# Style steps spread over ScalarE, gamma's last steps on GpSimd and one z tile on VectorE, in an adapter and mixture-of-experts kernel

## The reference

```python
# layer 0: an adapter, chosen per sample
hidden = gelu(x @ down_W.T + down_b)
hidden = hidden @ expert_W[id].T + expert_b[id] + domain_emb[id]
x1 = layernorm(hidden @ up_W.T + up_b + x) * ln_gamma + ln_beta
# layer 1
h = layernorm(x1) * ln_g + ln_b
h_norm = (h - mean_over_tokens(h)) * rsqrt(var_over_tokens(h) + 1e-8)
se = subj_emb[subject_ids]
hyp = relu(se @ hyp_w1 + hyp_b1) @ hyp_w2 + hyp_b2
sty = relu(hyp @ sty_w1 + sty_b1) @ sty_w2 + sty_b2
gamma, beta = split(sty, 2)
h = h_norm * (softplus(gamma) + 1e-8) + beta
# top 2 of 8 experts; each expert: relu(h @ w1 + b1) @ w2 + b2, 128 -> 512 -> 128
out = x1 + sum over experts of gate * expert(h)
```

## Time and profile before

| | |
|---|---|
| median of 3 runs | 119.39 us (118.95 to 119.65) |
| the profiled execution | 119.94 us, span of its program 118.2 us |
| PE busy | 112.0 us (95%) |
| DVE busy | 91.8 us (78%) |
| ACT busy | 84.3 us (71%) |
| POOL busy | 54.1 us (46%) |
| chain that ended last | PE 72%, DVE 14%, ACT 5%, DMA 3%, POOL 1% |

### The profile page before, as it was taken

One profiled execution on the slowest core, in us unless ns is written; L12 is line 12 of the kernel. 1 busy time (PEld: TensorE's weight loads), 2 busy tenths in 40 slices (PEclk: granted clock), 3 DMA queues, 4 the chain that ended last, 5 costly groups with the idle time before them and its releaser, 6 DMA issues.

```text
span 118.2 us, 1665 instructions
## 1 busy us (share of the span) xinstructions
PE 112.0 (95%) x519; PEld 84.3 (71%) x519; DVE 91.8 (78%) x228; ACT 84.3 (71%) x153; POOL 54.1 (46%) x75
## 2 busy tenths in 40 slices
PE   6799988999999999999999999999999999999990
PEld 2157534777777888688888888888888888888780
DVE  4486988999899989997685959595867777776772
ACT  2139845698999988697878787878778687878400
POOL 5020889226417000101259999976758941322310
PEclk9999999999999999999999999999999999999999
DMA  4939699994000000326999300000000000000005
GB/s 68 343 97 365 173 374 442 384 412 150 0 0 3 0 6 0 89 100 165 415 446 408 169 0 6 0 0 0 0 0 0 0 0 0 6 0 0 0 0 178
DMA packets 4473, 14.17 MB, mean 120 GB/s; under 512 B 561, under 2 KB 1905, under 8 KB 4209
## 3 DMA queue, kind: packets, MB, share of 16 engines
q1 hardware_dynamic: 3024, 9.67, 21.9%
q0 software_dynamic: 1008, 3.67, 8.8%
q10 hardware_dynamic: 432, 0.73, 2.2%
HBM read 13.52 MB, written 0.56 MB: 119 GB/s over the span
## 4 chain that ended last, share of the span: by engine, by line
PE 72%; DVE 14%; ACT 5%; issue 3%; DMA 3%; POOL 1%; DVEq 0%; ACTq 0%; POOLq 0%
PE bank L594 22%; PE bank L595 22%; PE bank L633 12%; PE bank L613 11%; DMA ids_i<-ids_dram 3%; DVE x L913 2%; ACT hid_high L508 2%; DVE stats L920 1%; ACT bank L511 1%; DVE hid_low L1005 1%; DVE bank L905 1%; POOL z L370 1%; PE bank L750 1%; DVE stats L876 1%; PE bank L583 1%
## 5 line engine op out<-in xcount | busy, mean ns | idle before, releaser
L508 ACT ACTIVATE hid_high<-bank,early_sb 128x512 fp32r<-128x512 f32 x64 | 44.2, 691 | 15.9 <-PE bank L613 15.8
L1005 DVE TENSOR_TENSOR hid_low<-bank,hid_high 128x512 fp32r<-128x512 f32 x51 | 34.8, 687 | 16.7 <-ACT bank L511 16.1
L511 ACT ACTIVATE bank<-bank,early_sb 128x512 f32<-128x512 f32 x51 | 33.6, 658 | 0.0
L308 POOL TENSOR_TENSOR w_low<-w_raw,w_high 128x256 fp32r<-128x256 f32 x32 | 22.7, 734 | 12.3 <-DMA w_high<-w_all_dram 4.4
L633 PE MATMUL bank<-hid_low,w_high 128*128 128x512 f32 x64 | 25.9, 405 | 0.4 <-DVE hid_low L1010 0.2
L594 PE MATMUL bank<-h_high,w_low 128*128 128x512 f32 x64 | 25.5, 398 | 0.3 <-ACT h_high L486 0.3
L594 PE MATMUL bank<-hid_high,w_low 128*128 128x512 f32 x64 | 25.6, 400 | 0.0
L595 PE MATMUL bank<-h_high,w_high 128*128 128x512 f32 x64 | 25.3, 396 | 0.0
L613 PE MATMUL bank<-h_low,w_high 128*128 128x512 f32 x64 | 25.1, 397 | 0.0
L595 PE MATMUL bank<-hid_high,w_high 128*128 128x512 f32 x64 | 25.0, 390 | 0.0
L318 POOL TENSOR_TENSOR y_sum<-y_sum,y_part 128x512 f32<-128x512 f32 x9 | 11.6, 1292 | 17.3 <-DVE y_part L1025 15.1
(11 more groups left out here) (136 smaller groups left out, 99.2 us busy)
## 6 DMA issues: line engine op xcount, KB each, us to landing
w_high<-w_all_dram POOLq DMA_DIRECT2D x7, 512.0 KB, 7.9
w_raw<-w_all_dram SPq DMA_DIRECT2D x1, 2560.0 KB, 10.9
gate_all<-gate_scratch SPq DMA_DIRECT2D x4, 512.0 KB, 5.9
gate_all<-gate_scratch SPq DMA_DIRECT2D x1, 2048.0 KB, 12.5
w_raw<-w_all_dram SPq DMA_DIRECT2D x3, 512.0 KB, 3.9
style_sb<-style_dram SPq DMA_DIRECT2D x1, 324.0 KB, 5.6
tables_sb<-tables_dram ACTq DMA_DIRECT2D x1, 272.0 KB, 3.8
xT_sb<-xT_dram SPq DMA_DIRECT2D x1, 256.0 KB, 4.4
```

Of the source, the lines that this page charges most:

```text
L308: nc.gpsimd.tensor_tensor(w_low[:, e % W_RING, quarter(q)], w_raw[:, e, quarter(q)], w_high[:, e % W_RING, quarter(q)].bitcast(F32), ALU.s ...
L508: ac(hid_high[:, slot, :], hid_ps[slot][:, :], ACT.Relu, bias=bias).then_inc(relu_steps, 1)
L511: ac(hid_ps[slot][:, :], hid_ps[slot][:, :], ACT.Relu, bias=bias).then_inc(relu_steps, 1)
L1005: v.tensor_tensor(low, ps, high.bitcast(F32), ALU.subtract).then_inc(low_vector, 1)
```

## The change

Four things are changed; all else is as before.

- Style: the steps of hyp1 and hyp2 go from VectorE to ScalarE. ScalarE now takes hyp1, weight quarter 0, hyp2, quarter 1, sty1, quarter 2, gamma_raw, and rounds quarter 3 only behind the soft logarithm. On VectorE the one step left, se_T, is behind `token_mv(0, 0, HB)`, and `centre(1)` and `adapter_out(1)` are ahead of `x1_stats(0)`.
- gamma: ScalarE writes a second tile, gamma_relu = max(g, 0). GpSimd does the rest of the softplus in four small steps, behind its z tiles and ahead of quarter 3 of expert 0. VectorE's t_gain waits for all four (`gamma_steps`).
- z: tile 3 (`normalise(T + 1)`) is made on VectorE instead of ScalarE.
- ScalarE's order behind gamma_raw: the root of sample 0, gamma_relu, beta_T, the root of sample 1, then the soft exponential and logarithm. minus_abs waits for gamma_raw alone.

```diff
@@ gpsimd
+            def softplus():
+                pool.wait_ge(gamma_relu_ready, 1)
+                pool.wait_ge(soft_ln, 1)
+                nc.gpsimd.tensor_tensor(gamma_T[:, :], gamma_relu[:, :], soft[:, 2, :], ALU.add).then_inc(gamma_steps, 1)
+                pool.wait_ge(gamma_steps, 1)
+                nc.gpsimd.tensor_scalar(gamma_T[:, :], gamma_T[:, :], 1e-8, None, ALU.add).then_inc(gamma_steps, 1)
+                pool.wait_ge(gamma_steps, 2)
+                nc.gpsimd.tensor_scalar(minus_gamma[:, :], gamma_T[:, :], -1.0, None, ALU.mult).then_inc(gamma_steps, 1)
+                nc.gpsimd.tensor_scalar(gamma_g[:, :], gamma_T[:, :], col(C_LNG), None, ALU.mult).then_inc(gamma_steps, 1)
...
-            split_lows(0)
+            split_lows(0, (0, 1, 2))
             normalise(0, T)
+            softplus()
+            split_lows(0, (3,))
             split_lows(1, (0, 1))
@@ scalar
             token_root(0, tiles(0, 2))
-            round_first_weights((0, 1, 2))
+            act.wait_ge(style_in_psum, 2)
+            ac(hyp1_T[:, :], hyp1_ps, ACT.Relu, bias=col(C_HB1)).then_inc(style_ready, 1)
+            round_first_weights((0,))
+            act.wait_ge(style_in_psum, 3)
+            ac(hyp2_T[:, :], hyp2_ps, ACT.Identity, bias=col(C_HB2)).then_inc(style_ready, 1)
+            round_first_weights((1,))
             act.wait_ge(style_in_psum, 4)
             ac(sty1_T[:, :], sty1_ps, ACT.Relu, bias=col(C_SB1, SC)).then_inc(style_ready, 1)
-            round_first_weights((3,))
+            round_first_weights((2,))
             act.wait_ge(style_in_psum, 6)
             ac(gamma_raw[:, :], gam_ps, ACT.Identity, bias=col(C_SBG)).then_inc(gamma_beta_ready, 1)
+            token_root(1, tiles(0))
+            ac(gamma_relu[:, :], gam_ps, ACT.Relu, bias=col(C_SBG)).then_inc(gamma_relu_ready, 1)
             ac(beta_T[:, :], bet_ps, ACT.Identity, bias=col(C_SBB)).then_inc(gamma_beta_ready, 1)
-            token_root(1, tiles(0))
+            token_root(1, tiles(1))
             soft_exponential()
-            token_root(1, tiles(1))
             soft_logarithm()
-            normalise(T + 1)
+            round_first_weights((3,))
             feature_root(0)
@@ vector
                 after(("f_mean", h))
+                ve.wait_ge(gamma_steps, 4)
                 v.scalar_tensor_tensor(t_gain[:, bs], t_off[:, bs], col(C_LNB), minus_gamma[:, bs], ALU.subtract, ALU.mult
...
-            style_step(0)
             token_mv(0, 0, HB)
-            style_step(1)
+            style_step()
             ve.wait_ge(ln0_loaded, 16)
             centre(0)
-            style_step(2)
+            centre(1)
             adapter_out(0)
-            centre(1)
+            adapter_out(1)
             x1_stats(0)
-            adapter_out(1)
...
-            softplus(0)
-            softplus(1)
-            softplus(2)
+            normalise(T + 1)
```

More of the change, by code:

```diff
@@ L138, in adapter_moe @@
         gamma_raw = sb("gamma_raw", [P, B])
+        gamma_relu = sb("gamma_relu", [P, B])
         beta_T = sb("beta_T", [P, B])
@@ L215, in adapter_moe @@
         gamma_beta_ready = sem("gamma_beta_ready")
+        gamma_relu_ready, gamma_steps = sem("gamma_relu_ready"), sem("gamma_steps")
         soft_in, soft_exp, soft_ln = sem("soft_in"), sem("soft_exp"), sem("soft_ln")
@@ L219, in adapter_moe @@
         z_affine, z_ready, zT_in_psum = sem("z_affine"), sem("z_ready"), sem("zT_in_psum")
-        z_vector, z_scalar = sem("z_vector"), sem("z_scalar")
+        z_vector = sem("z_vector")
         scale_ready, affine_ready, h_ready = sem("scale_ready"), sem("affine_ready"), sem("h_ready")
@@ L474, in soft_logarithm @@
                 ac(soft[:, 2, :], soft[:, 1, :], ACT.Ln, bias=1.0).then_inc(soft_ln, 1)
[L476 to L479, removed]
             def round_h(h):
@@ L580, in transpose_z @@
                 if b != 2:
-                    pe.wait_ge(*((z_vector, 1), (z_scalar, 1), None, (z_vector, 2))[b])
+                    pe.wait_ge(z_vector, (1, 2, None, 3)[b])
                 for t in range(T):
@@ L821, in _, with style_step @@
                             ).then_inc(up_eff_ready, 1)
[L824 to L832, removed]
+            def style_step():
+                ve.wait_ge(style_in_psum, 1)
+                v.tensor_copy(se_T[:, :], se_ps).then_inc(style_ready, 1)
             def minus_abs():
-                ve.wait_ge(gamma_beta_ready, 2)
+                ve.wait_ge(gamma_beta_ready, 1)
                 v.scalar_tensor_tensor(soft[:, 0, :], gamma_raw[:, :], -1.0, gamma_raw[:, :], ALU.mult, ALU.min
                                        ).then_inc(soft_in, 1)
[L839 to L854, removed]
             mark = {}
```

## The result

The changed kernel takes 121.56 us (median of 6 runs) against 119.25 for the kernel before in the same measurement: 1.019 times as long, with an interval of 1.0155 to 1.0225. Measured once more in another batch it was 1.0162 times as long, 1.0113 to 1.0211. It is slower by 1.6 to 1.9%, some 1.8 to 2.3 us. Two of the six executions had a mean granted clock of 0.96 and 0.97 and took 122.86 and 122.23 us; the median of the other four is 121.25, 2.0 us above the kernel before. The forecast was +0.5 us, and 121.56 lies above its range, which ends at 120.6.

What follows compares the result with a forecast made beforehand. TensorE's nearly gapless matmuls from about 20 us bound the kernel, so only their start, set by the chain to h_low, counts. -0.31 + 0.36 + 0.41 = +0.46 us gives 119.9 us (forecast 119.6 to 120.15, range 118.9 to 120.6).

Steps and rivals of the forecast that it cites:

- The first term, -0.31: Front of the kernel: statistics of zT of sample 1 start at 16.77 instead of 17.08, -0.31 us.
- gamma_raw comes at 13.94, 0.25 late: Style chain: with hyp1 and hyp2 on ScalarE, gamma_raw ends at 13.94 instead of 13.69.
- paid from time that VectorE won: Root of sample 0: its early VectorE input absorbs the style chain's delay; root ends at 14.63 against 14.75.
- The holds on the affine step: Running w_low on GpSimd stretch VectorE's t_gain (second term, +0.36 us) and scale_T (third term, +0.41).
- Held to 20.75, again 0.24: h_low of sample 0: held beside a w_low by 0.24 us as already before, so no added cost.
- the rival of the split pair: A w_low gets in between the two h_low, the second waits another 0.6: +1.1, 120.5 us; chance 0.18.
- other move at nothing: Moves counted as free: later quarter 3 and w_low of expert 1, loads issued 1.2 us later, gamma_relu on ScalarE.
- the one-to-one carry: From h_low to the kernel's end: any shift of h_low moves the end by the same amount.
- the covers of the loads and of quarter 3: GpSimd's later loads (covered by 0.3 us) and quarter 3 (there by 19.05, needed at 21.29) delay nothing.
- the wait for the gamma steps costs nothing: GpSimd's gamma steps are done at 16.95, t_gain needs them at 17.84: covered by 0.9 us.
- nothing is held: No w_low stretches t_gain or scale_T, so only the first -0.31 us stays: 119.1 us; chance 0.20.
- the rival of the late style chain: ScalarE's style steps stick behind weight quarters, gamma_raw after 14.3, front gain gone: +0.8, 120.2 us; chance 0.08.

Runs made afterwards that it cites:

- b_quarter_behind_z: Kernel before, with only GpSimd's w_low of quarter 3 moved behind its z tiles: 119.41 us, ratio 1.0019.
- b_lows_behind_h: Kernel before, with GpSimd's w_low of quarter 3 and the four of expert 1 held until h_low is done: 118.69 us, ratio 0.9946.
- c_style_vector: Changed kernel with the style steps back on VectorE and the five late w_low held until h_low is done: 119.55 us, 0.9997 to the kernel before.
- a_h_low_free: Changed kernel, with only the last two w_low of expert 1 waiting for h_low: 120.34 us, 1.0096 to the kernel before.

## Why the prediction was wrong

**The first term, -0.31, came out at -0.02.** The step that failed is "gamma_raw comes at 13.94, 0.25 late": it came 0.60 late (+4.59 against +3.99), 0.35 behind the forecast. ScalarE's first step began at 11.42, 0.03 behind the end of rstd, where I had put it 0.11 behind its start; a product that TensorE had to wait for took 0.39 us, not 0.28; and from the end of sty_T to gamma_raw it was 0.81 instead of 0.72. From gamma_raw on ScalarE has no idle time up to the root of sample 1, whose log_var starts at +5.48, where the forecast (14.86) has +5.16. Its input from VectorE was there at +5.21. The statistics of sample 1 then come at +7.36 instead of +7.07. So "paid from time that VectorE won" failed: VectorE had the input of the root of sample 0 ready at +4.11, near the forecast's +4.03, but that root stood behind gamma_raw until +4.76.

The other links of this term held. soft without its hold is worth 0.36 us of path where it stands ahead of the root of sample 1 (b_quarter_behind_z, b_lows_behind_h). z of tile 3 on VectorE costs 0.05, as I had it (0.06). Putting the style steps back on VectorE gives only 0.08, since VectorE is then the late one (c_style_vector).

**The holds on the affine step were seen, and sized at 0.77 for 1.04.** t_gain and scale_T went as forecast. The step that failed is that I listed only operations with two SBUF inputs. t_off has one, and its output in SBUF, and was held for 0.28 us; in the kernel before it met only the last 0.1 us of a w_low, which did not tell. The place of the w_low was off too: the gamma steps, of 0.20 to 0.29 us instead of my 0.19, were done 0.54 us behind the statistics of sample 1 and not 0.18. By my place the first w_low would have ended 0.87 behind them, and t_off starts 0.7 behind: by the 0.26 us at which it went on before a w_low's end, an estimate, it would have passed. The Trainium skill, SBUF — State Buffer, "Who interferes with whom", says that copy, cast and tensor_scalar can enter a mode that uses both ports and contends with GpSimd, when their operands allow it; t_off is a tensor_scalar, and 0.57 us against 0.28 with its output in PSUM fits. But the gamma steps of the kernel before are tensor_scalar as well and ran plain beside GpSimd's z (0.17 and 0.23 us), which had misled me; what sets t_off apart from them no run here shows.

**"Held to 20.75, again 0.24" for h_low was wrong: the rival of the split pair was right.** I gave it a chance of 0.18. The w_low that was ready took its turn between the two h_low, which then cost 0.63 more together than before. a_h_low_free shows it: 0.75 us of path return with these two w_low alone. The Trainium skill, in the same page under "SBUF: two separate sides", says that whoever starts first has the pair for its whole instruction; the trace agrees, with a second w_low of 0.94 us and a second h_low of 0.95.

**The end of the kernel had no term.** The diff's one line `gamma_relu = sb(...)` moved every later tile by 16 bytes, z among them, and cost 0.22 us at the stores. No "other move at nothing" mentioned it. Against the forecast the misses are 0.29 in the first term, 0.27 in the affine step, 0.63 at h_low, 0.03 on the way and 0.22 at the end: 1.44 us on +0.46 make +1.90.

**Right:** the one-to-one carry (+1.25 us at the end of h_low by the spans' clocks, +1.28 at the last step), the covers of the loads and of quarter 3, and that the wait for the gamma steps costs nothing: done at 17.20, ahead of t_gain at 17.95. The rival "nothing is held" fell with the first trace. The rival of the late style chain was right about its effect, the gain of the front gone: gamma_raw came at +4.59, which is 14.29 on the clock of before, at the edge of its condition. It was wrong about the reason, since no style step on ScalarE stood behind a weight quarter: hyp1 came 0.03 behind the root's rstd, and the others 0.04 behind the product that they needed.

## What to carry to other kernels

Where GpSimd runs beside VectorE, a change of GpSimd's order has to be read against VectorE's list: which of its operations have two SBUF inputs (or are of the single-input kind that was held here), and what stands next to them. Let GpSimd wait for the end of such a stretch, and let it issue DMAs meanwhile; here such an order alone gave 0.4 to 0.5%, while moving one operand to PSUM only passed the hold on. Before a step moves to another engine, look at what stands behind it in that engine's list: here the root stood behind gamma_raw. Allocate a new small tile behind the large ones that DMAs read and write: 16 bytes ahead of them cost 0.22 us here.

## What the runs showed of the hardware

- A VectorE operation of 2 columns (plain 0.16 to 0.29 us) beside w_low took 0.52 to 0.82 us: less its plain length, each went on 0.13 to 0.26 us before a w_low's end. The same with an operand in PSUM took 0.22 and 0.28.
- Where both engines have such operations pending, they alternate, one instruction each: w_low 0.94, h_low 0.95.
- Moving the tiles behind gamma_raw by 16 bytes, the one that the output is stored from among them, made stores of 128 KB land in 2.1 us instead of 1.9. The Trainium skill, DMA: Bandwidth & Descriptors, "How a descriptor splits into AXI transactions", says that a transfer which doesn't start on a 256-byte boundary fetches from the boundary below it; that this is the cause here no run shows, as only this one shift was tried.
- Still open: which of the moved tiles makes the stores late, and why t_off is held beside w_low and the gamma steps are not beside GpSimd's z.
